# Exp at the exit of the transposed scores, and experts' rows, weights and biases fetched apart, in a four-layer attention kernel with a mixture of experts

## What is computed

```python
scores = jnp.einsum('bhqd,bhkd->bhqk', q, k) / jnp.sqrt(jnp.float32(dh))
attn = jax.nn.softmax(scores, axis=-1)
out = jnp.einsum('bhqk,bhkd->bhqd', attn, v)
...
h1 = jax.nn.gelu(jnp.einsum('nd,efd->enf', hf, fc1_w) + fc1_b[:, None, :], approximate=False)
eo = jnp.einsum('enf,edf->end', h1, fc2_w) + fc2_b[:, None, :]
```

## Time and profile before

| | |
|---|---|
| runs | 3736.32, 3720.77, 3734.92 us |
| profiled execution | 3734.74 us, of which the span is 3732.9 |
| TensorE busy | 3195.7 us, 86% |
| VectorE busy | 2605.4 us, 70% |
| ScalarE busy | 2652.3 us, 71% |
| GpSimd busy | 1246.9 us, 33% |
| mean granted TensorE clock | 0.952 of full speed |

### The profile page before, as it was taken

The page is one execution under the profiler, slowest core; times in us unless marked ns, Lnnn a source line. Parts: engine busy times, 40 slices in busy tenths (PEclk is TensorE's granted clock), DMA queues, the critical chain, the costliest instruction groups (busy, mean ns, idle before and its releaser), DMA issues.

```text
span 3732.9 us, 87645 instructions
## 1 busy us (share of the span) xinstructions
PE 3195.7 (86%) x30064; PEld 2269.6 (61%) x30064; DVE 2605.4 (70%) x5408; ACT 2652.3 (71%) x5088; POOL 1246.9 (33%) x1615
## 2 busy tenths in 40 slices
PE   6898888888888979998988888998888997777897
PEld 3566556566756657665665656666565665665565
DVE  7877787755477777556888777665888877326775
ACT  4777777777876757887776766788776776656566
POOL 3122333212153353112244244212235434214632
PEclk9999999999999989999999999999999998989899
DMA  7013200134410033221000014322000004442000
GB/s 280 1 43 135 109 6 15 30 97 108 103 37 3 18 100 89 69 64 43 19 22 14 3 44 109 83 72 57 26 23 20 6 19 108 103 112 59 16 2 13
DMA packets 211920, 212.98 MB, mean 57 GB/s; under 512 B 51808, under 2 KB 155168, under 8 KB 211232
## 3 DMA queue, kind: packets, MB, share of 16 engines
q1 hardware_dynamic: 203296, 190.58, 18.1%
q0 software_dynamic: 8192, 16.79, 1.5%
HBM read 135.98 MB, written 71.30 MB: 56 GB/s over the span
## 4 chain that ended last, share of the span: by engine, by line
PE 39%; DVE 23%; ACT 15%; issue 8%; SPq 7%; DMA 4%; POOL 4%; ACTq 0%; DVEq 0%; POOLq 0%
PE ps L1933 8%; DVE mx L2320 6%; PE ps L1923 5%; PE ps L1945 4%; DVE pr L2326 4%; DMA b_up<-cols 4%; ACT block_hid L2211 3%; ACT pt L2164 3%; PE ps L1892 3%; PE ps L1953 2%; PE ps L2005 2%; PE ps L1918 2%; DVE kx L2326 2%; ACT xh L2114 2%; SPq L1818 1%
## 5 line engine op out<-in xcount | busy, mean ns | idle before, releaser
L2320 DVE TENSOR_REDUCE mx<-ps 128x8 f32<-128x616 f32 (+1 forms) x704 | 671.4, 954 | 334.7 <-PE ps L1923 316.4
L2164 ACT ACTIVATE pt<-ps 77x512 f32<-77x512 f32 (+1 forms) x1408 | 768.9, 593 | 126.1 <-PE ps L1933 123.2
L2576 POOL TENSOR_TENSOR kx<-kT,in_tiles 128x308 f32<-128x308 f32 (+1 forms) x384 | 315.7, 822 | 830.5 <-PE ps L1923 740.0
L1933 PE MATMUL ps<-k_sb,pr 128*77 128x128 f32 (+1 forms) x3776 | 538.9, 284 | 33.9 <-ACT pr L2155 10.3
L1933 PEld LDWEIGHTS ps<-k_sb,pr 128*77 128x77 f32 (+1 forms) x3776 | 421.1, 147 | 142.2 <-issue 73.2
L1945 PE MATMUL ps<-pt,v 77*16 77x128 f32 (+2 forms) x11264 | 444.3, 278 | 29.0 <-ACT pt L2164 11.2
L2326 DVE TENSOR_TENSOR pr<-ps,mx 128x616 f32<-128x616 f32 (+1 forms) x472 | 450.3, 954 | 16.2
L2155 ACT ACTIVATE pr<-pr 128x616 f32<-128x616 f32 (+1 forms) x472 | 392.7, 840 | 75.6 <-DVE pr L2326 74.6
L2173 ACT ACTIVATE og<-ps 128x256 f32<-128x256 f32 x704 | 267.3, 381 | 236.8 <-PE ps L1945 233.6
L1923 PE MATMUL ps<-kx,qT 32*128 32x308 f32 (+2 forms) x2816 | 361.6, 547 | 42.2 <-ACT pt L2164 15.8
L1945 PEld LDWEIGHTS ps<-pt,v 77*16 77x16 f32 (+2 forms) x11264 | 251.8, 97 | 181.1 <-issue 85.1
(11 more groups left out here) (209 smaller groups left out, 5733.3 us busy)
## 6 DMA issues: line engine op xcount, KB each, us to landing
w_up<-weights SPq DMA_DIRECT2D x160, 256.0 KB
w_down<-weights SPq DMA_DIRECT2D x160, 256.0 KB
sent<-block_hid SPq DMA_DIRECT2D x42, 512.0 KB, 6.3
made<-block_hid SPq DMA_DIRECT2D x42, 512.0 KB, 6.3
block_rows<-sent SPq DMA_DIRECT2D x160, 64.0 KB
b_down<-expert_b SPq DMA_DIRECT2D x160, 64.0 KB
made<-block_out SPq DMA_DIRECT2D x160, 64.0 KB, 2.2
cT<-ctx_cols SPq DMA_DIRECT2D x32, 154.0 KB, 3.1
```

Source lines behind the costliest of these rows:

```text
L1933: i = tr(p[0:keys, j * L:(j + 1) * L], probs[s][pl.slot(unit, 3)][:, c:c + keys], ident)
L2164: go_act(pt[s][0:keys, q % 2, :], p[0:keys, :], ACT.Copy).then_inc(probsT_ready.sem, 1)
L2320: link(v_.tensor_reduce(m, tile, AX.X, ALU.max, negate=True))
L2576: tell(pool, g_.tensor_tensor(spread_keys[s][:, pl.slot(step, 2), 0:4 * keys].rearrange("p (h k) -> p h k", h=4), kT[s][:, b * keys:(b + 1 ...
```

## The change

1. **Exp.** `soft` has no part on ScalarE any more. VectorE's shifted scores are transposed as they are, and the copy out of PSUM applies Exp with the scale. The same 704 units, the same 1408 exits from PSUM.
2. **Fetches.** `take` is split. `fetch` brings the rows of a pair, and waits only for `block_turn` of the pair before. `take` (now one for each block) brings `w_up` and `b_up`, and waits for `block_up` of the same block in the pair before to be done on TensorE, no longer for Gelu; `b_up` has two buffers. `take_down` brings `w_down` after `block_down` of the pair before has been made, and `b_down` after VectorE has added. Each has a semaphore of its own, and registers are loaded ahead of the wait instead of behind it. `block_turn` of the next pair now stands ahead of `block_down` of this one.
3. **Order.** The planner's costs and tables have new numbers, so each engine has a new list.

```diff
@@ expert_steps
-        out += [("block_turn", g, p), ("block_up", g, p, 0), ("block_up", g, p, 1)]
-        out += [("take", g, p + 1)] if p + 1 < PAIRS else []
+        more = p + 1 < PAIRS
+        out += [("fetch", g, p + 1)] if more else []
+        for j in range(2):
+            out += [("block_up", g, p, j)] + ([("take", g, p + 1, j)] if more else [])
+        out += [("block_turn", g, p + 1)] if more else []
         out.append(("block_down", g, p))
@@ parts
-    if kind == "take":
-        return [(Y, 1.2)]
+    if kind in ("fetch", "take"):
+        return [(Y, 0.5)]
...
-        return [(V, 2.52 if t.own else 1.67), (A, act(8 * keys, 0.5))]
+        return [(V, 2.52 if t.own else 1.67)]
...
@@ tables
-TABLE = {"soft": "exp", "route": "exp", "step_size": "exp", "decay": "exp", "block_up": "gelu", "hidden": "tanh",
+TABLE = {"turn": "exp", "route": "exp", "step_size": "exp", "decay": "exp", "block_up": "gelu", "hidden": "tanh",
-STAY = 0.6307
-EAGER = {"apply": {A: 0.0298}, "bias": {G: -17.4648}, "bias_mlp": {G: 42.9269}, "block_down": {V: 0.196},
+STAY = 0
+EAGER = {"apply": {A: 0.0298}, "bias": {G: -18.0823}, "bias_mlp": {G: 42.9269}, "block_down": {V: 0.5989},
...
@@ build, SyncE
-                elif kind == "take":
+                elif kind == "fetch":
...
+                    at = [nc.sync.value_load(row_of[0:1, g, n:n + 1], min_val=0, max_val=2 * REGION - L) for n in (2 * p, 2 * p + 1)]
...
                     if former:
-                        sp.wait_ge(*up_made(*former, 1))
-                        sp.wait_ge(*up_ready(*former, 1))
...
+                        sp.wait_ge(*block_turned(*former))
+                    for j, row in enumerate(at):
+                        sp.dma_start(block_rows[:, j, :], sent[bass.ds(row, L), :]).then_inc(rows_fetched, 16)
+                elif kind == "take":
+                    g, p, j = step[1:]
...
+                    e = nc.sync.value_load(expert_of[0:1, g, n:n + 1], min_val=0, max_val=NE - 1)
+                    if former:
+                        sp.wait_ge(*up_made(*former, j))
+                    sp.dma_start(w_up[:, j, :], weights[:, bass.ds(e * FF + W_FC1, FF)]).then_inc(ups_taken[j], 16)
+                    sp.dma_start(b_up[:, p % 2, j, :], cols[:, bass.ds(e * FC + C_AT["L1_fc1_b"][0], FC)]).then_inc(ups_taken[j], 16)
@@ build, TensorE
-                    pe.wait_ge(*probs_ready(*unit[1:]))
+                    pe.wait_ge(*scores_shifted(*unit[1:]))
...
-                    pe.wait_ge(blocks_taken, 6 * 16 * in_order(g, q))
+                    pe.wait_ge(rows_fetched, 2 * 16 * in_order(g, q))
...
                     pe.wait_ge(*block_ready(g, q))
+                    pe.wait_ge(ups_taken[j], 2 * 16 * in_order(g, q))
@@ build, ScalarE
-                elif kind == "soft":
...
-                    act.wait_ge(*scores_shifted(*args))
-                    v = probs[s][pl.slot(step, 3)][:, 0:8 * keys]
-                    go_act(v, v, ACT.Exp, scale=t.scale).then_inc(probs_ready.sem, 1)
...
-                    go_act(pt[s][0:keys, q % 2, :], p[0:keys, :], ACT.Copy).then_inc(probsT_ready.sem, 1)
+                    go_act(pt[s][0:keys, q % 2, :], p[0:keys, :], ACT.Exp, scale=t.scale).then_inc(probsT_ready.sem, 1)
```

More of the change, by code:

```diff
@@ L650 @@
[L650 removed]
+         "store": {G: 10.8306, Y: -17.6682}, "table": {V: 27.3959}, "take": {Y: -21.1819},
+         "take_down": {Y: -7.0216}, "turn": {P: 0.0003, A: -0.1517}, "turn_gate": {P: 0.3214, A: 27.106},
+         "turn_out": {P: 0.032, A: -0.0214}, "values": {P: 60.8532, V: 30.3777}, "weigh": {G: -24.1984},
          "z": {A: -0.1633}}
@@ new lines @@
+    {"STAY": 4.7055, "block_down": {P: 0.3752}, "block_turn": {A: -1.1986}, "block_up": {P: -0.2683},
+     "clear": {Y: -41.2385}, "context": {Y: -26.4244}, "count": {V: -0.122}, "decay": {P: -7.4139},
+     "gate_norm": {G: 38.9893}, "gather": {G: -14.0397}, "keep": {Y: -8.7671},
+     "mamba_out": {P: 2.5364, V: 11.5188}, "mlp": {P: 0.0736}, "out": {V: 0.666}, "rope": {P: -0.0499, V: -0.7918},
+     "route": {A: 2.3865, P: 4.0433, V: 21.2326}, "rows": {P: 7.1719, V: 6.9529}, "step_size": {A: 0.0534},
+     "take_down": {Y: 3.1929}, "turn": {P: 0}, "turn_gate": {A: 9.5278, P: 0.6818}, "values": {V: 22.9219},
+     "weigh": {G: -24.5328}, "z": {P: -1.3707}},
@@ new lines @@
+    {"block_turn": {A: -0.1077, P: -2.9981}, "clear": {Y: -41.4832}, "context": {Y: -25.9617},
+     "conv": {P: -1.1018}, "count": {V: -0.122}, "decay": {A: 5.2895, P: -1.0672}, "gather": {G: -13.0288},
+     "give": {Y: -3.1042}, "keep": {Y: -6.0254}, "out": {P: 0.2514, V: 0.0235}, "project": {A: 1.3267},
+     "route": {A: -0.6705, V: 18.7674}, "rows": {P: 7.41}, "spread": {G: -1.3381},
+     "step_size": {A: 0.0534, V: 40.5797}, "step_size2": {V: -6.9787}, "take_down": {Y: 3.2662},
+     "turn": {P: 0.8989}, "turn_gate": {A: 17.367, P: 0.6818}, "values": {P: 63.6157, V: 33.1402},
+     "weigh": {G: -22.7739}},
@@ new lines @@
+    {"block_down": {P: 3.2043}, "clear": {Y: -41.4832}, "context": {Y: -19.5157},
+     "conv": {A: 2.8105, P: 2.5495, V: 2.7907}, "count": {P: 0.1914, V: 0.0804}, "decay": {A: -0.6677},
+     "keep": {Y: -6.3459}, "mlp": {V: 1.8378}, "out": {V: 0.0235}, "pairs": {P: -1.29, V: -3.1296},
+     "project": {A: 5.5544}, "reload": {Y: 43.7342}, "route": {A: -0.7656}, "rows": {P: 7.41}, "scan": {G: 2.6902},
+     "stats": {G: -0.1907}, "step_size": {A: -1.0509}, "step_size2": {V: -0.3192}, "store": {G: 11.5989},
+     "take": {Y: -20.9057}, "take_down": {Y: 3.8714}, "turn": {P: 0}, "turn_gate": {A: 20.6417, P: -0.2585},
+     "values": {P: 60.8274, V: 30.3519}, "weigh": {G: -24.5328}},
```

1696 lines of the change are left out of this document (904 added, 792 removed).

## The result

The changed kernel takes 3789.72 us, the median of 4 runs (3777.42 to 3796.99); beside it on the same chip the kernel before took 3735.62. The ratio is 1.0148, 95% interval 1.0108 to 1.0187: 54 us slower. The prediction was 3600, faster. The direction was wrong.

A forecast was written before the change was run, and what follows sets the result against it. It took TensorE's work plus its 537 us standing still to bound the kernel. 3732.9 - 42 (fetch) - 85 (ScalarE) - 8 (clock) = 3598, with 1.8 around it 3600 us; own range 3510 to 3670, widened to 3490 to 3700.

The forecast's parts named there:

- What bounds: Whole span: TensorE's 3195.7 us of work plus 537 us standing still; a change helps as far as it shortens the latter.
- The price of Exp: ScalarE: dropping the pass saves 588 us of work, leaving 2064; exits cost the same under Exp, with 235 table loads.
- I take 85: TensorE's 236 us of waits for ScalarE: relieving ScalarE gives back 85 us, chosen between 52 and 118.
- at the least 52, as its work falls: TensorE's waits for ScalarE: lower bound of their fall, 22% like ScalarE's work, 52 us.
- The second rival: VectorE takes ScalarE's place: only the fetch's 42 us and few ScalarE waits come back, about 3685 us; chance 0.13.
- So a pair can't come faster than every 11.0 us.: SyncE's queue in the experts' stages: 12 DMAs and 8 register loads take 11.0 us for one pair.
- The third rival: SyncE's queue loop: waits chain, a pair takes 14 us, +132 us, 3815 us in all; chance 0.08.
- the fetch's term: Experts' stages: splitting and moving the fetches saves 42 us, 17 in stages 0 and 3, 25 in stages 1 and 2.
- The other edits of this part come at nothing.: Fetch part: later `b_down`, `block_turn` ahead of `block_down` and a second `b_up` cost nothing.
- The moved work: TensorE in stages 0 and 3: 9.6 and 8.4 us a pair remain; moved work adds 10 and 6 us idle elsewhere.
- The clock: TensorE's granted clock, mean 0.952: less waiting gives back 8 us of a possible 30.
- the first rival: All waits go: 108 us of fetch, 118 of ScalarE's and 30 of clock, 3479 us; chance 0.10.

The follow-up runs named there:

- runs 5 and 6: Exp in place of the experts' Gelu: in the kernel before, 3701.81 us; in the kernel before with Exp at the exits, old lists, 3697.73 us.
- Run 8: Changed kernel with the next pair's rows fetched ahead of `take_down` and `give` on SyncE's queue, nothing taken out: 3691.94 us, ratio 0.9902 to the kernel before.
- run 4: Changed kernel, its steps and planner's costs kept, with the planner's tables of priorities from the kernel before: 3947.3 us, ratio 1.0576.
- run 2: Kernel before with the fetch edit alone, other engines' lists as before and Exp as before: 3615.25 us, ratio 0.9696.
- run 12: Changed kernel with rows fetched ahead of `take_down` and `give`, and no bias fetches after the first pairs: 3616.2 us, ratio 0.9709 to the kernel before.
- run 3: Kernel before with both the Exp and the fetch edit, all lists of steps as before: 3657.32 us, ratio 0.9806.
- run 1: Kernel before with the Exp edit alone, every engine's list and the fetches as before: 3757.4 us, ratio 1.0074.

## Why the prediction was wrong

**What bounds.** TensorE plus its idle was the right frame, and the 54 us split cleanly in it: 36 by clock, 18 by idle.

**The price of Exp.** Exits at 588 and 595 ns and 235 loads came as forecast. ScalarE's busy time is 2158 us, not 2064: the rows of its groups add to 2834.8 us before, though it was busy 2652.3, since neighbouring instructions overlap in the rows. The pass was 588 us as rows and 494 as busy time. This did no harm.

**"I take 85" for ScalarE's relief.** This step failed. The forecast let the 236 us of waits shrink with ScalarE's load, to about 150. They became 213, and in the old lists runs 5 and 6 give 4 us for 483 us of relief, where few table loads disturb; at most some 22 us are compatible with them, under the forecast's lowest, 52. The likely reason, which no run isolates, is that ScalarE's results are late because their inputs are late: with a lighter load it waits longer (233.6 to 571.7 us) for TensorE's mixed heads. The bound "at the least 52, as its work falls" was no bound. The first paragraph of the prediction had said that freeing ScalarE is worth nothing by itself; the sum then gave it 85. The second rival had this half right, though VectorE did not take over either: its waits stayed at 142.

**"So a pair can't come faster than every 11.0 us."** As a floor this holds wherever all 12 DMAs are kept. The step that failed is taking the floor for the period. The period was 13.5 and 12.6 us, because the queue waited for `block_down` 41.6 and 17.5 us. The third rival had named the place, "`fetch` stands behind `give` of the pair before", a price, +132 us at 14 us a pair, and the point from which it decides, 12.7 us a pair, and was given 0.08. The mean of the two periods is 13.0. Run 8 removes the ring and nothing else and returns 98 us (92 by the ratios). What is left, 3692, is near what the fetch's term alone would have given, 3735 - 42 = 3693, in part by chance: against the kernel before, run 8 has 33 us less idle and 12 us less busy time, and the term was 42 of idle.

**"The other edits of this part come at nothing."** Wrong for one of them, as far as the runs go. `block_turn` ahead of `block_down` makes `block_down` of this pair wait for the rows of the next, and so is a link of the ring. The new steps have the ring with either numbers (changed kernel, run 4); the old steps with the same queue order have none (run 2), and gain 113 us. That it is this link and no other difference of the lists wasn't tried with the link alone.

**The moved work.** Packing was forecast at 9.6 and 8.4 us of TensorE a pair; run 12 has 9.3 and 8.3 at nearly full clock. Right, and it is why the new order needs a faster queue than it has: the old one had 12.5 and 9.9 us of work beside 11 of the queue.

**The clock.** Forecast as a gain of 8 us; it fell to 0.936. In stage 0 it is 0.87 where TensorE stands 22% of the time, 0.94 before at 16%, and 1.00 in run 2 at 9%. The same 2356 matrix instructions took 251.92 us there before and 236.79 in run 2. Idle in the experts' stages is thus paid twice.

**The sum again.** 3600, with 85 for ScalarE and 8 for the clock not given, and 98 for the ring, is 3791; measured 3790. That it meets so closely is partly luck: half of the 98 is clock, the 85 is struck out on runs in the old lists, and by the ratios the 98 is 92.

**The range.** Its low end, 3510, doesn't follow from its terms: -108, -118 and -30 from 3735 are 3479, the first rival's time, and 3510 leaves the 30 of clock out. The stated range started at 3490, and the miss was at the other end.

**Open.** Run 8 is 35 us slower than run 3, which has the same code in the old lists. The queue's 11 us against 9.3 and 8.3 of work fits that, but no run separates it from the rest of the new lists. What Exp at the exits is worth in the new lists, which were made for it, wasn't tried either, nor the old lists with the turn alone moved ahead of the down.

## What to carry to other kernels

Before a fetch is split or moved, write down the ring that it stands in: from its issue through landing and consumer to whatever must end before the queue reaches the next one. A step moved on another engine can close that ring. Compare three numbers per round, the ring, the queue's own work and the bound engine's work. The period is at least the largest of them, and longer where a closed ring meets uneven work, as here (11 us for the ring and the queue, 13.5 and 12.6 measured). Moving independent work out of a stage helps only until the last falls below the others. An engine that isn't the bound may give next to nothing back when it is relieved, even if the bound engine shows waits for it (here 4 us for 483): look first at its own waits, whether its inputs come late.

## What the runs showed of the hardware

- The table loads at the exits started after the wait of the exit, not during it (run 1: 29.5 us of idle ahead of 93 loads). The Trainium skill (ScalarE: Activation LUTs, What ACT_TABLE_LOAD costs) has 1283 ns for the load, and that is the mean in every group of loads in these runs.
- SyncE's queue costs 11 us for 12 DMAs and 8 register loads, some 0.53 us from issue to issue. Now and then an issue takes 1 us or more: two of `b_down` took 1.88 us in stage 0 at 882.67 where others took 0.85.
- From issue to landing (part 6 of the page; KB for each, then us):

```profile
w_up<-weights SPq DMA_DIRECT2D x160, 256.0 KB, 2.6
block_rows<-sent SPq DMA_DIRECT2D x160, 64.0 KB, 1.9
```

The 2.6 us agree with the estimate of the prediction by the Trainium skill (DMA: Bandwidth & Descriptors, Anatomy of one DMA). That section gives its fixed 2.0 us for DMAs issued by GpSimd, and these are SyncE's, so the agreement may be chance; the 1.9 us lie under the fixed 2.0 alone.
